# A fused attention and mixture-of-experts kernel on one core: the first group's start and the last group's order changed

## What is computed

```python
# 8 batches; the 256 rows are 32 heads (h) of 8 channels (i, j); l runs over the 512 columns, L = 512
kv = einsum('bhil,bhjl->bijhl', k, v)                 # k = v = ctx
y = irfft(rfft(kv, 2L) * rfft(ssm_kernel, 2L))[..., :L] + kv * D
x = x + einsum('bijhl,bhil->bjhl', y, layernorm(x))
n = layernorm(x)
scores = softmax(n @ gate_w.T); w, i = top_k(scores, 4); w = w / w.sum(-1)
# each expert takes its first 256 tokens: silu(n @ w_gate) * (n @ w_up) @ w_down, times w
x = x + sum_over_chosen_experts + silu(n @ sw_gate) * (n @ sw_up) @ sw_down
```

## Time and profile before

| | before |
|---|---|
| median of 3 runs | 620.4 us |
| profiled execution | 620.51 us, span 618.4 us |
| TensorE busy | 586.6 us (95%), 4387 matmuls |
| VectorE busy | 487.8 us (79%) |
| GpSimd busy | 396.7 us (64%) |
| ScalarE busy | 291.6 us (47%) |
| DMA | 92.01 MB, mean 149 GB/s |

### The profile page before, as it was taken

How to read it: one execution, slowest core, us unless ns; L and a number is a source line. 1 busy time by engine, 2 the same in 40 slices (tenths; PEclk the granted TensorE clock), 3 DMA queues, 4 the chain that set the end, 5 groups by cost and what they waited for, 6 DMA issues and landing times.

```text
span 618.4 us, 13645 instructions
## 1 busy us (share of the span) xinstructions
PE 586.6 (95%) x4387; PEld 549.2 (89%) x4387; DVE 487.8 (79%) x1277; ACT 291.6 (47%) x521; POOL 396.7 (64%) x502
## 2 busy tenths in 40 slices
PE   3969999999999999999999999999999999999993
PEld 3759988999999989989999797999999999999992
DVE  6988787679779779598698878988888788887640
ACT  2525334434434435345261333666665566566741
POOL 6997988878888888789771363178834433333342
PEclk9989999999999999999999999999999999999997
DMA  6575215136325336152340146778887888888643
GB/s 189 182 249 170 72 69 166 49 85 179 82 80 156 75 93 170 42 140 55 85 111 2 51 160 209 231 246 233 222 239 211 216 237 237 240 226 241 147 53 48
DMA packets 60489, 92.01 MB, mean 149 GB/s; under 512 B 4260, under 2 KB 36004, under 8 KB 60440
## 3 DMA queue, kind: packets, MB, share of 16 engines
q1 hardware_dynamic: 53168, 74.53, 39.4%
q0 software_dynamic: 7168, 16.78, 13.3%
q10 hardware_dynamic: 104, 0.08, 0.1%
HBM read 74.29 MB, written 17.08 MB: 148 GB/s over the span
## 4 chain that ended last, share of the span: by engine, by line
PE 76%; DVE 9%; POOL 6%; issue 4%; ACT 2%; DVEq 1%; DMA 1%; POOLq 0%; SPq 0%; ACTq 0%
PE gu L678 16%; PE gu L827 15%; PE yb L558 11%; PE mb L844 10%; PE gu L716 7%; PE yb L827 6%; PE mb L530 4%; POOL kv L1230 3%; PE yb L530 2%; PE yb L608 2%; DVE oT L1507 2%; DVE prod L1489 2%; DVE prod L1491 1%; POOL kvl L1247 1%; PE yb L798 1%
## 5 line engine op out<-in xcount | busy, mean ns | idle before, releaser
L678 PE MATMUL gu<-xT,sw 128*128 128x256 f32 (+2 forms) x1104 | 136.4, 281 | 0.3 <-issue 0.3
L678 PEld LDWEIGHTS gu<-xT,sw 128*128 128x128 f32 (+2 forms) x1104 | 131.8, 180 | 1.0 <-issue 0.7
L1230 POOL TENSOR_TENSOR kv<-kT 128x256 f32 (+3 forms) x232 | 106.8, 500 | 0.0
L1247 POOL TENSOR_TENSOR kvl<-kv,kvh 128x1440 fp32r<-128x1440 f32 (+1 forms) x28 | 87.7, 3132 | 25.8 <-ACT kvh L954 25.6
L1489 DVE TENSOR_TENSOR prod<-yb,qT 128x64 f32<-128x64 f32 (+10 forms) x272 | 74.8, 286 | 16.4 <-PE yb L608 11.4
L954 ACT ACTIVATE kvh<-kv 128x1440 fp32r<-128x1440 f32 (+1 forms) x28 | 37.5, 1339 | 78.9 <-POOL kv L1237 36.9
L1507 DVE TENSOR_REDUCE oT<-prod 128x256 f32<-128x2048 f32 x32 | 73.0, 2280 | 0.1
L558 PE MATMUL yb<-kvh,tlast 128*128 128x288 f32 x280 | 66.0, 297 | 0.0
L1491 DVE TENSOR_TENSOR prod<-yb,qT 128x96 f32<-128x96 f32 (+10 forms) x238 | 64.2, 270 | 0.0
L844 PE MATMUL mb<-ed,midh 128*128 128x512 f32 x180 | 57.4, 400 | 0.0
L1776 DVE TENSOR_TENSOR ew<-raw_w,ew 128x704 fp32r<-128x704 f32 x64 | 55.1, 882 | 0.3 <-ACT ew L1102 0.3
(11 more groups left out here) (219 smaller groups left out, 1327.4 us busy)
## 6 DMA issues: line engine op xcount, KB each, us to landing
raw_w<-in_L_ffn_w_gate_dram SPq DMA_DIRECT2D x16, 704.0 KB, 7.9
raw_w<-in_L_ffn_w_up_dram SPq DMA_DIRECT2D x16, 704.0 KB, 8.8
raw_d<-in_L_ffn_w_down_dram SPq DMA_DIRECT2D x16, 512.0 KB, 4.3
tlast<-toeplitz_taps SPq DMA_DIRECT2D x20, 384.0 KB, 3.5
tstep<-tap_steps SPq DMA_DIRECT2D x20, 256.0 KB, 4.1
c_t<-in_ctx_dram SPq DMA_DIRECT2D x16, 256.0 KB, 4.8
x_t<-in_x_dram SPq DMA_DIRECT2D x16, 256.0 KB, 4.9
toep<-toeplitz_taps SPq DMA_DIRECT2D x8, 512.0 KB, 3.9
```

The lines of the kernel that those rows point to most:

```text
L678: last = pe.matmul(bank[0:m, u * GT:(u + 1) * GT], sw[:, c, a, col:col + m], xT[:, c, b, :], start=(c == 0 and (a, b) == PASSES[0]), stop= ...
L1230: last = pool.tensor_tensor(to[:, :, POFF[d]:POFF[d] + w], src[:, :, 0:w], src[:, :, d * B:HD * B], ALU.mult)
L1247: pool.tensor_tensor(kvl[:, s, 0:nb, :], kv[:, s, 0:nb, :], kvh[:, s, 0:nb, :].bitcast(fp32), ALU.subtract)\
```

## The change

Start of the kernel:

- SyncE loads x of group 1 right behind that of group 0, into a semaphore of its own; the taps and the skip weights get one each.
- GpSimd makes the three index constants first, then the padding's zeros, the identity and the rest.
- VectorE makes the nine mask instructions ahead of the taps. It takes the statistics of group 1 right behind its pair products.
- The tap steps are made by GpSimd (two subtractions, later the low part) and ScalarE (the rounding copy), before they touch kT.
- ScalarE executes one dummy copy before the taps, so that its table is loaded there.
- Pair products of head 0 wait for the first tile of kT alone, and GpSimd computes the rate of x after three of its five.
- TensorE multiplies the identity with itself, into a part of `gu` that nobody reads: five times before the first transposes, sixteen times before head 0's convolution. Head 0's `between` (the transposes of x) comes after block 0.

All groups but group 0: `mixed_out` waits for the head sums tile by tile. In group 1, tile 0 is transposed inside head 4's convolution, tile 1 after it.

Last group: tile 0's `mixed_out` and `add_x` come before head 31; tile 1's after three pieces of the down product; rates come behind `low_tokens`. The clearing of `xg` is moved behind the second `weights`. `slots(1)` is moved behind most of the last down product; VectorE's order around it changes (middles and low parts first, then the one-hot, the decode and the rows of expert 0, then places and values); ScalarE's silu comes one piece earlier.

```diff
             load_group(0, parts="c")
             load_group(0, parts="x")
+            load_group(1, parts="x")
             sp.dma_start(gate_rows[:], gate_w).then_inc(gate_in, 16)
...
-            sp.wait_ge(x_stat, 1)
-            load_group(1, parts="x")
...
-            def mixed_out(g, nq):
-                pe.wait_ge(d_sum, GH * (g + 1))
-                for t in range(TT):
+            def mixed_out(g, nq, tiles=range(TT)):
+                for t in tiles:
                     wait(pe, q_ev, TT * nq + t + 1)
+                    pe.wait_ge(d_sum, GH * g + (t + 1) * GH // TT)
...
-                    convolve(GH * g, 0, lambda: mixed_out(g - 1, g))
+                    convolve(GH * g, 0, lambda: mixed_out(g - 1, g, [0]))
+                    mixed_out(g - 1, g, [1])
...
+                if not prep:
+                    mixed_out(g, g, [0])
                 convolve(GH * g + 3, 3)
...
-            pe.wait_ge(consts, 2)
+            def idle_products(count):
+                for _ in range(count):
+                    pe.matmul(gu[:, 1, 0:P], ident[:], ident[:], start=True, stop=True)
+
+            pe.wait_ge(consts, N_IDENT)
+            idle_products(5)
             prep_ctx(0)
-            convolve(0, 0, lambda: prep_q(0))
+            idle_products(16)
+            convolve(0, 0, lambda: prep_q(0), 1)
...
-            mixed_out(NG - 1, NG - 1)
-            down(NG - 2, [0])
+            down(NG - 2, [0], range(-1, 1))
+            mixed_out(NG - 1, NG - 1, [1])
+            down(NG - 2, [0], range(1, SJ - 1))
...
-            slots(1)
             down(NG - 1, [0])
             down(NG - 1, [1], range(-1, 2))
+            slots(1)
             rows_t(0, 0)
...
+            act.wait_ge(consts, N_HALF)
+            act.activation(ready[:], half_neg[:, 0:1], ACT.Copy)
             act.wait_ge(pad_whole, 1)
             act.dma_start(first_dram, pad[0:GH, :]).then_inc(first_out, 16)
+            act.wait_ge(steps_d, 2)
+            act.activation(stephl[:, 0, :, :], steps_of[:], ACT.Copy).then_inc(steps_h, 1)
...
-                if i > 1:
-                    silu(NG - 1, i)
+                if 0 < i < SJ - 1:
+                    silu(NG - 1, i + 1)
                 round_mid(NG - 1, i)
...
-            pool.wait_ge(k_ev, TT)
-            for d in range(3, HD):
+            pool.wait_ge(pad_whole, 1)
+            pool.tensor_tensor(steps_of[:, 0, :], pad[:, 0:2 * P], pad[:, P:3 * P], ALU.subtract).then_inc(steps_d, 1)
+            pool.tensor_tensor(steps_of[:, 1, :], pad[:, 2 * P:4 * P], pad[:, P:3 * P], ALU.subtract)\
+                .then_inc(steps_d, 1)
+            pool.wait_ge(steps_d, 2)
+            pool.wait_ge(steps_h, 1)
+            pool.tensor_tensor(stephl[:, 1, :, :], steps_of[:], stephl[:, 0, :, :].bitcast(fp32), ALU.subtract)\
+                .then_inc(steps_hl, 1)
+
+            pool.wait_ge(k_ev, 1)
+            for d in range(FIRST_POOL, HD):
+                if d == HD - 2:
+                    inverse_x(0)
...
             weights(1)
+            pool.wait_ge(conv, H)
+            pool.wait_ge(d_sum, H)
+            pool.wait_ge(o_tr, TT * NG)
+            pool.wait_ge(n_l, TT * NG)
+            for k in range(2):
+                pool.memset(xg[k][:], 0.0).then_inc(xg_zero, 1)
+            pool.wait_ge(xg_zero, 2)
             low_mid(NG - 1, 1)
...
+                    if hl == 2 and not prep:
+                        add_x(g, [0])
...
             steps(NG - 1, False)
-            add_x(NG - 1)
+            add_x(NG - 1, [1])
             choose(0)
-            rates(0)
             chunk_sum(NG - 2, [0])
             low_tokens(NG - 1)
+            rates(0)
             chunk_sum(NG - 2, [1])
...
             middle(NG - 1, 2)
+            middle(NG - 1, 3)
             rank_of(2, E)
-            one_hot(1)
-            middle(NG - 1, 3)
             low_mid(NG - 1, 2)
             low_mid(NG - 1, 3)
-            decode(1, 1)
             middle(NG - 1, 4)
+            middle(NG - 1, 5)
             low_mid(NG - 1, 4)
-            middle(NG - 1, 5)
             low_mid(NG - 1, 5)
+            one_hot(1)
             low_w(0, 0, 2)
             low_w(0, 0, 3)
             chunk_sum(NG - 1, [0])
+            decode(1, 1)
+            low_rows(0, 0)
             places(2, 4)
             values(2, 4)
             places(4, 10)
-            low_rows(0, 0)
             chunk_sum(NG - 1, [1])
```

More of the change, by code:

```diff
@@ L115, in xattn_moe_kernel @@
         warm = place("warm", [P, 1], fp32)
+        ready = place("ready", [P, 1], fp32)
         half_neg = place("half_neg", [P, TT], fp32)
@@ L372, in load_group @@
                     if "x" in parts:
+                        landed = x_more if isinstance(g, int) and g == 1 else x_in
                         sp.dma_start(x_t[:, bass.ds(g % 3, 1), t, :].rearrange("p s l -> p (s l)"),
-                                     x_g[g, t]).then_inc(x_in, 16)
+                                     x_g[g, t]).then_inc(landed, 16)
             def load_toep(n, k):
@@ L592, in convolve @@
                             last.then_inc(conv_half, 1)
-                        if between:
+                        if between and at_block == LB // 2:
                             between()
                         free(n, 1)
+                    elif between and lb == at_block:
+                        between()
                     bank, at = home(n, lb // 2)
@@ L1365, in _ @@
             weights(0)
-            pool.wait_ge(conv, H)
-            pool.wait_ge(d_sum, H)
-            pool.wait_ge(o_tr, TT * NG)
-            pool.wait_ge(n_l, TT * NG)
-            for k in range(2):
-                pool.memset(xg[k][:], 0.0).then_inc(xg_zero, 1)
-            pool.wait_ge(xg_zero, 2)
             def gather(e, k):
@@ L1439, in split_shared, with stats @@
                     last.then_inc(sw_l, 1)
-            def stats(tile, st, mv, ve, nm, signal):
-                for t in range(TT):
+            def stats(tile, st, mv, ve, nm, signal, tiles=range(TT)):
+                for t in tiles:
                     dve.bn_stats(st[:, t, :], tile(t))
+                if TT - 1 not in tiles:
+                    return
                 dve.drain()
@@ L1458, in prep_stats @@
             def prep_stats(g):
-                dve.wait_ge(x_in, 32 * g + 32)
+                if isinstance(g, int) and g == 1:
+                    dve.wait_ge(x_more, 32)
+                else:
+                    dve.wait_ge(x_in, 32 * g if not isinstance(g, int) or g else 32)
                 wait(dve, x_rs, g)
@@ L1509, in add_up, with add_x @@
                     .then_inc(d_sum, 1)
-            def add_x(g):
+            def add_x(g, tiles=range(TT)):
                 if isinstance(g, int) and g == 0:
@@ L1538, in middle @@
                 wait(dve, mid_l, (SJ - 1) * g + (min(max(i - 2, 0), 1) if last_group else max(i - 2, 0)))
+                if last_group and i > 3:
+                    dve.wait_ge(last_l, i - 3)
                 if i == 2:
@@ L1652, in first_steps @@
             def first_steps():
-                add_x(0)
+                add_x(0, [0])
+                add_x(0, [1])
                 multiply(GH, 1, 0)
@@ L1723, in _ @@
             link(dve.tensor_tensor(own_b[:], before_in_b[:], same_b[:], ALU.subtract))
[L1724 to L1728 removed]
+            dve.wait_ge(taps_in, 16)
+            dve.wait_ge(pad_ok, 1)
+            link(dve.tensor_copy(pad[:, 0:L], tap_rows[:, ::-1]))
+            dve.wait_ge(skip_in, 16)
+            dve.tensor_tensor(pad[:, L - 1:L], pad[:, L - 1:L], skip_t[:], ALU.add).then_inc(pad_whole, 1)
+            dve.wait_ge(pad_whole, 1)
+            link(dve.tensor_copy(padhl[:, 0, :], pad[:]))
+            dve.tensor_tensor(padhl[:, 1, :], pad[:], padhl[:, 0, :].bitcast(fp32), ALU.subtract).then_inc(taps_hl, 1)
+            prep_stats(0)
+            dve.wait_ge(k_ev, 1)
+            for d in range(FIRST_POOL):
+                w = (HD - d) * B
+                last = dve.tensor_tensor(kv[:, 0, 0:LB, POFF[d]:POFF[d] + w], kT[:, 0, :, 0:w],
+                                         kT[:, 0, :, d * B:HD * B], ALU.mult)
+            last.then_inc(kv0_m, 1)
+            prep_stats(1)
             dve.wait_ge(steps_hl, 1)
             dve.wait_ge(first_out, 16)
[L1731 removed]
             head(0, 0, 0)
```

44 lines of the change are left out of this document (15 added, 29 removed).

## The result

| | us, median (lowest to highest) | ratio to before, 95% |
|---|---|---|
| before, same chip | 620.83 (619.65 to 621.54) | |
| after | 618.57 (616.47 to 620.88) | 0.9958 [0.9949, 0.9967] |
| predicted | 615.0 (612.9 to 618.0) | |

What follows compares the result with a forecast made beforehand. TensorE, busy 586.6 of 618.4 us, was the bound, with early losses set by VectorE's and GpSimd's chains. Gains of 3.6 + 1.4 + 0.45 = 5.4 us from the median 620.4 gave 615.0 us, range 612.9 to 618.0.

Steps and rivals of the forecast that it cites:

- The last group: Last group: TensorE's idling near 344 and 354 us goes, 1.4 us; at the handover to expert 1, 0.45 us survives.
- wait for `ew`: Before expert 1: TensorE's wait for VectorE's ew grows from 0.55 us to about 2.
- Rivals A and E: Handover: A, gather 1 lands late, 616.3 to 617, chance 0.14; E, VectorE blocks GpSimd's memsets, 621.7, chance 0.03.
- The split: Group 0's mixed_out by tile: TensorE's 4.29 us idle goes, statistics near 43.8 to 44.0, 4.3 us sooner.
- x of group 1 is now in the queue ahead ... I take no delay, at most 1.5 us: Start: the 512 KB take 2 us of transfer ahead of the first taps; no delay taken, at most 1.5 us.
- Rival B: First group: idle products at half clock or taps 2 us late, 616.7, with GpSimd's steps 617.7; chance 0.18.
- The steps on GpSimd: Start: tap steps take roughly 0.6 + 0.6, 0.5, 1.2 us and fill GpSimd's wait for kT, 5.3 to 8.3.
- The clock: Before conv 0: idle products raise TensorE's clock by 7.8 us and end at 10.1 to 10.9, before the taps.
- Head 0 starts on DVE at 13.7, not 18.2: First group: VectorE starts head 0 at 13.7 instead of 18.2 us; head 0 ends 3.1 us sooner.
- the port rule: Memsets of the last group: ports shared by VectorE and GpSimd are held a whole instruction, the other blocks fully.
- POOL's rate at once, 44.7: First group: GpSimd's gapless run ends near 44.7 us, rate computed at once, against 48.41; a gain of 3.7 us.
- the 3.6 us: First group: TensorE leaves 97 us about 3.6 us sooner.

Runs made afterwards that it cites:

- last_only: The kernel before with only the last group's edits; 618.97 us, ratio 0.9968.
- split_last: last_only plus group 1's mixed tokens transposed by tile and add_x a tile at a time, no other first-group edits; 617.51 us, ratio 0.9955.
- dve_steps: The changed kernel with the tap steps back on VectorE behind its part of kv0; 618.18 us, ratio 0.995.
- late_x: The changed kernel with x of group 1 loaded behind the first taps and the store of the tap rows; 619.37 us, ratio 0.9986.
- idle32: The changed kernel with 32 idle products instead of 16 before conv 0; 618.78 us, ratio 0.9962.
- norm_idle: The changed kernel with 14 idle products added ahead of the transposes of normalised tokens at 51.7 us; 618.71 us, ratio 0.9961.
- best2: late_dve_steps with 20 idle products, group 1's statistics between head 0's halves, places of experts 4 to 9 behind the first expert unit; 618.63 us, ratio 0.9972.
- late_dve_steps: The changed kernel with x of group 1 loaded behind the taps and the tap steps back on VectorE; 616.29 us, ratio 0.9932.
- late_dve_no_idle: late_dve_steps without any idle product; 617.1 us, ratio 0.9945.
- best2_ps: best2 with the two 128x2 tensor_scalars behind each group's statistics moved from VectorE to GpSimd; 615.03 us, ratio 0.9908.
- late_x_ps: late_x with the two 128x2 tensor_scalars behind each group's statistics moved from VectorE to GpSimd; 616.48 us, ratio 0.9937.

## Why the prediction was wrong

Point by point, by its steps.

**The last group: right.** 1.4 + 0.45 forecast, 1.9 measured (`last_only`), with the wait for `ew` (1.68 us there, "about 2" forecast) and memsets at full speed. Rivals A and E did not come. The two terms were not measured apart.

**The split: right in mechanism.** The statistics follow the second half of head 0 by 26.6 instead of 27.9 us, and `split_last` measures 1.5 us by the medians, 0.8 by the ratios.

**"x of group 1 is now in the queue ahead ... I take no delay, at most 1.5 us": wrong, the first step that failed.** The transfer was costed as bytes in front of the load of the taps. In front of that load stands the store of the same taps, 10 KB, issued at 4.97 us into queues that hold two groups of x; it took 5.2 us instead of 2.35. SP's wait for it turns this into 2.6 us for the taps: 13.96 instead of 11.34. That the landing of this store is on the way to the taps could be seen in the trace of before, as the distance between two issue rows (5.29 and 7.64). Rival B, at 0.18, named this delay with "the taps land 2 us late" and priced it at 616.7 to 617.7; the mechanism came, and the median lies 0.9 us above its upper end.

**The steps on GpSimd: mis-sized.** 0.6 + 0.6 + 0.5 + 1.2 became 0.94 + 1.30 + 0.63 + 1.26 with 0.80 us of waiting around ScalarE's copy, so they ended at 9.4 instead of 8.3. The forecast took 2.4 ns a column from a split of 128x704; two subtractions of 32x256 took 1.1 us each. Why is not shown: VectorE was busy with the same padding at that time, and its own 32x640 subtraction took 1.23 us instead of 0.82. This is a full microsecond on kv0. It cost nothing in after, where the taps are later still (`dve_steps`), nor in `late_x`.

**The clock: half right.** The idle products brought it to 2.4 GHz as forecast. That it holds until conv 0 was assumed, because no gap was expected. With 3.42 us of idling it fell, and the records at half clock cost VectorE's chain 3.1 us in the profiled execution: from the start of conv 0 to VectorE's second half it is 8.98 us, against 5.93 in `idle32`. How long it stays down differs: in `norm_idle` the same gap (3.06 us) was followed by 4.63 us for the eighteen records, not 6.16, and the second half came at 21.05. The prediction cited a rule on this (TensorE: Matmul & The Clock Gate of the Trainium skill, "What's actually happening": the phase of the observation is free-running, so that slow stretches vary) and weighed it for the block of idle products only, not for the gap behind it. This is the part of after's spread that the runs show best, by the correlation with the granted clock.

**"Head 0 starts on DVE at 13.7, not 18.2": wrong by 5.4 us, by the late taps and the clock.** VectorE idles 4.37 us there, so taking masks and steps from it bought time that nothing could use. The masks cost nothing where they are, as forecast.

**The price of a small instruction beside GpSimd: not in the sum, and not shown to matter in after.** The prediction used the port rule for the memsets of the last group, where nothing came of it. In the first group VectorE's statistics of group 1 stand beside pair products, and in one execution of `best2` a two-column instruction took 3.30 us. In after's own profile the two took 0.40 and 0.56 us instead of 0.16, and VectorE idled 4.37 us behind them: a stall shorter than that would have cost nothing there. In `late_x` and `best2` nothing is idle behind them.

**POOL's rate at once, 44.7: wrong.** It came at 49.80 after 2.17 us of waiting. GpSimd's own run ended late as well, at 47.6, having waited 1.69 us for kT behind the slow conv 0. (The pairs of head 1 did fall from 4.53 to 3.50 us, as forecast.) `late_dve_steps` shows the rate at 46.45 after 0.56 us. A part of the 3.6 us was there to be had: that kernel gives 2.7 us on `last_only` by the medians, 2.2 by the ratios.

The size, then. The last group gave its 1.9 us. Of the 3.6 us of the first group the median has about 0.4. The shortest executions say where the rest is. An estimate from rows: with the taps at 13.96 and the 5.93 us that `idle32` has at full clock, VectorE's second half would begin at 19.9, near the 19.6 of `late_dve_steps`; and after's shortest executions (616.47 to 617.10, at the highest clock) are where that kernel's median is (616.29). So the late taps cost little by themselves. They make the gap in which the clock falls in some executions and not in others, and this takes up to 4.4 us. That the clock is what differs between the executions is inferred from the granted clocks; the profile shows one execution of each kernel, in after's case the longest.

The last 1.3 us to 615.0 are missing even without that. The forecast has taps at 11.3, x of group 1 landed before 10.6 and the second half at 17.2. No run had both. With x first, the taps come at 13.3 to 14.0 (the six profiles in which TensorE waits for them); with the taps first, VectorE gets x of group 1 at 14.5 to 14.9, and its second half begins at 19.4 to 19.7 (`late_x`, `late_dve_steps`, `late_dve_no_idle`). `best2` goes round this by taking the statistics between the halves of head 0.

`best2_ps` is the fastest, 615.03 us against 620.92 of before in the same set and 618.57 of after.

## What to carry to other kernels

Before a bulk load is moved ahead in a queue, look for small stores behind it whose landing something waits for: what they lose is the price. Idle products keep TensorE's clock only if nothing opens a gap behind them, so price that gap with the clock lost. Before work is taken off an engine, look at what that engine waits for next; here it was PE's conv 0, which the same change made later. When a change widens the spread, set the times of all executions against their granted clocks first. Only where they don't go together, as in `best2`, look for one short instruction of VectorE with twenty times its usual duration beside a gapless run of GpSimd.

## What the runs showed of the hardware that was not expected

- A 128x2 tensor_scalar of VectorE took 3.30 us instead of 0.16, in one execution of `best2`, beside sixteen GpSimd products of 0.44 us each on the mean: it ran across seven or eight of them. `BATCH_NORM` instructions and products with an operand in PSUM kept their durations in the same stretch (0.25 and 0.46 to 0.47 us).
- The granted clock was 0.58 to 0.60 in 13 to 14 us after 1.88 us of idling in one kernel and 3.42 in another, and stayed at 1.00 after 1.23, 1.33 and 1.63 us in three others (`late_dve_steps`, `late_x`, `late_x_ps`).
- A store of 10 KB was followed by the load that waits for it after 2.2 to 3.4 us with one group of x in front (twelve profiles), after 4.6 to 5.4 us with two (eight profiles).
